# Scatters in pairs and singly between the splits' operations, a reordered filling stage, and one ACT write for both choices' rows

## The reference

```
x = layernorm(x + attn(x))       # 16 heads of 8, q/k/v through V (8x8), softmax over 512 keys, back through U and Wo
x = layernorm(x + ffn(x))        # gate: softmax over 8 experts, top 2, renormalised
                                 # expert: relu(x @ w1.T + b1) @ w2.T + b2, hidden size 512
```

## Time and profile before

| | |
|---|---|
| median of 3 runs | 1258.94 us (1251.39 to 1264.15) |
| the profiled execution: time | 1257.38 us |
| its span, first to last instruction | 1255.6 us |
| mean granted clock of PE | 0.939 |
| busy: PE, DVE, ACT, POOL | 86%, 78%, 72%, 47% of the span |
| first exponential scores (L553) / last | 76.3 / 904.6 us |
| L799 DVE row maxima | 512 of 1220 ns |
| L685 ACT exponentials | 512 of 1023 ns |

### The profile page before, as it was taken

The page is one execution under the profiler, slowest core; times in us unless marked ns, Lnnn a source line. Parts: engine busy times, 40 slices in busy tenths (PEclk is TensorE's granted clock), DMA queues, the critical chain, the costliest instruction groups (busy, mean ns, idle before and its releaser), DMA issues. The chain is left out here.

```text
span 1255.6 us, 24757 instructions
## 1 busy us (share of the span) xinstructions
PE 1082.8 (86%) x7711; PEld 520.5 (41%) x7711; DVE 975.3 (78%) x2117; ACT 904.2 (72%) x1177; POOL 586.5 (47%) x823
## 2 busy tenths in 40 slices
PE   3578998989889898898988999888728999999977
PEld 2222222222222222222222222222218999999952
DVE  4578888989778797887988879797146888888845
ACT  1157877778677786867878678687618999999927
POOL 1314316255271642626336263323254777777745
PEclk9989999999899998989999899899758999999989
DMA  3733133141331413223142231400012222222246
GB/s 80 235 94 90 49 101 89 54 132 42 95 92 51 126 37 106 73 67 102 43 127 69 71 97 36 122 15 19 14 51 63 69 68 69 69 69 71 66 159 257
DMA packets 105461, 104.88 MB, mean 84 GB/s; under 512 B 21608, under 2 KB 82834, under 8 KB 105376
## 3 DMA queue, kind: packets, MB, share of 16 engines
q1 hardware_dynamic: 94912, 81.88, 22.5%
q0 software_dynamic: 8448, 16.93, 4.2%
q10 hardware_dynamic: 2016, 4.98, 1.1%
HBM read 56.06 MB, written 47.39 MB: 82 GB/s over the span
## 5 line engine op out<-in xcount | busy, mean ns | idle before, releaser
L799 DVE TENSOR_REDUCE row_max<-score_ps 128x2 f32<-128x1024 f32 x512 | 618.0, 1220 | 138.9 <-PE score_ps L571 91.3
L685 ACT ACTIVATE probs<-score_ps 128x1024 f32<-128x1024 f32 x512 | 521.6, 1023 | 157.4 <-PE score_ps L553 132.6
L534 PE MATMUL av_ps<-probs,v_one 128*9 128x512 f32 x2048 | 285.2, 630 | 7.9 <-ACT probs L685 6.5
L571 PE MATMUL score_ps<-k_stack,q_stack 48*128 48x512 bf16 x1024 | 207.5, 402 | 75.2 <-ACT probs L685 57.5
L553 PE MATMUL score_ps<-q_stack,k_stack 51*128 51x512 bf16 x1024 | 205.7, 399 | 22.0 <-DVE row_max L799 15.1
L371 POOL TENSOR_TENSOR max_parts<-neg_max,zeros 32x128 bf16<-32x128 f32 x32 | 14.2, 445 | 386.9 <-ACT neg_max L623 386.9
L1096 ACT ACTIVATE w_cur<-experts 128x1156 f32 x136 | 158.5, 1167 | 37.5 <-PEq L413 17.2
L553 PEld LDWEIGHTS score_ps<-q_stack,k_stack 51*128 51x128 bf16 x1024 | 49.2, 93 | 320.4 <-issue 154.2
L1192 POOL DMA_INDIRECT y_d<-y_out,place x136 | 136.8, 1006 | 44.7 <-issue 44.7
L846 POOL DMA_INDIRECT routed_d<-rows,slot_i x128 | 125.4, 980 | 67.2 <-issue 36.9
L1053 PE MATMUL up_ps<-xt_sb,w_cur 128*128 128x128 f32 x1088 | 146.2, 278 | 0.0
(11 more groups left out here) (187 smaller groups left out, 1153.3 us busy)
## 6 DMA issues: line engine op xcount, KB each, us to landing
k_stack<-k_stack_d SPq DMA_DIRECT2D x128, 96.0 KB, 2.4
q_stack<-q_stack_d SPq DMA_DIRECT2D x128, 96.0 KB, 2.5
x_rows_sb<-routed_d SPq DMA_DIRECT2D x136, 65.0 KB
q_stack_d<-q_parts SPq DMA_DIRECT2D x32, 192.0 KB
k_stack_d<-k_parts SPq DMA_DIRECT2D x30, 192.0 KB
x_in<-L_attn_x SPq DMA_DIRECT2D x16, 256.0 KB, 3.1
q_stack_d<-q_parts SPq DMA_DIRECT2D x32, 128.0 KB
x_res<-L_attn_x SPq DMA_DIRECT2D x16, 256.0 KB, 3.1
```

What stands on the lines that cost most here:

```text
L534: last = nc.tensor.matmul(av_ps[32 * g:32 * g + V_COLS, :], v_one[n.parity][:, kb, HG * hg + g, :], probs[:, (2 * j + g // 2) % P_RING, g ...
L571: last = nc.tensor.matmul(max_bank(b, s)[:, a, :], q_stack[n.parity][at, c, g * P:(g + 1) * P], k_stack[n.parity][at, c, :], start=True, s ...
L685: nc.scalar.activation(probs[:, s % P_RING, :, :], exp_bank(b, s)[:, :, :], ACT.Exp).then_inc(S["exp_done"], 1)
L799: nc.vector.tensor_reduce(row_max[:, m // (STEPS // 2), :, m % (STEPS // 2)], max_bank(b, s)[:, :, :], AX.X, ALU.max).then_inc(S["red_done ...
```

## The change

1. **Scatters.** On POOL scatters 0 and 1 now stand ahead of `split_max(b, 1)`, 2 and 3 right behind it, 4 between the second and third operation of q's split, 5 behind that split, 6 between the second and third operation of k's split and 7 behind it. None is left beside `split_max(n1, 0)`. The last batches, which have no q and k to split, have them in one piece.
2. **SP.** `max_rows(n1, 0)` is issued ahead of the wait for the stored parts and of `stacks(n2, 0)` and `(n2, 1)`.
3. **Filling stage.** The experts stand at steps 24 to 31, one in each step. The two banks have their own counts, so that PE can fill one while ACT copies the other. On POOL `split_max(0, 0)` comes between the splits of q and k of batch 1, and on SP its `max_rows` between their stores.
4. **ACT.** L617 writes both choices at once (input 128x128, output 128x256), in steps 18 to 21. The copy L671 and its semaphore are gone.

```diff
...

-EXPERT_AT = [STEPS - 2 * (E - e) for e in range(E)]
-SCALE_AT = 16
+EXPERT_AT = [STEPS - E + e for e in range(E)]
+SCALE_AT = 17
 LEAST = -3.0e38
...
          "xt_sb q_sb k_sb ynt_sb y_ready exp_done "
-         "x1t_done x1t_sb logits_done logits_sb second_sb top_step rank_done slot_step place_out copied "
+         "x1t_done x1t_sb logits_done logits_sb second_sb top_step rank_done slot_step place_out "
          "red_done negmax_sb yn_inv yn_sb v_sb res_ready stats_ready mv_ready x1_ready "
...

-def split(engine, queue, full, parts, rest_t, zeros, part_ready, value, last_sem):
+def split(engine, queue, full, parts, rest_t, zeros, part_ready, value, last_sem, between=None):

...
     engine.tensor_tensor(rest_t, full, parts[:, 0, :], ALU.subtract).then_inc(part_ready, 1)
+    if between:
+        between()
     queue.wait_ge(part_ready, value(2))
...

-def split_q(engine, queue, n):
+def split_q(engine, queue, n, between=None):
     queue.wait_ge(S["q_sb"], n.count(1, 1))
...
     wait(queue, S["split_done"], n.count(2, 0))
-    split(engine, queue, q_f[:, :], q_parts, rest[:, :], zeros[:, :], S["qpart_ready"], lambda k: n.count(3, k), S["split_done"])
-
-def split_k(engine, queue, n):
+    split(engine, queue, q_f[:, :], q_parts, rest[:, :], zeros[:, :], S["qpart_ready"], lambda k: n.count(3, k), S["split_done"], between)
+
+def split_k(engine, queue, n, between=None):
     queue.wait_ge(S["k_sb"], n.count(1, 1))
     queue.wait_ge(S["split_done"], n.count(2, 1))
-    split(engine, queue, k_f[:, :], k_parts, rest[:, :], zeros[:, :], S["kpart_ready"], lambda k: n.count(3, k), S["split_done"])
+    split(engine, queue, k_f[:, :], k_parts, rest[:, :], zeros[:, :], S["kpart_ready"], lambda k: n.count(3, k), S["split_done"], between)

...
                     pe.wait_ge(experts_loaded, 32)
+                wait(pe, experts_copied, 2 * e - 1)
+                for h in range(HB):
+                    last = nc.tensor.transpose(score_ps[2][:, 0, h * P:(h + 1) * P], w1_n[:, e * HB + h, :], ident[:, :])
+                last.then_inc(experts_ps, 1)
                 wait(pe, experts_copied, 2 * e)
                 for h in range(HB):
-                    nc.tensor.transpose(score_ps[2][:, 0, h * P:(h + 1) * P], w1_n[:, e * HB + h, :], ident[:, :])
                     last = nc.tensor.transpose(score_ps[2][:, 1, h * P:(h + 1) * P], w2_n[:, e, h * P:(h + 1) * P], ident[:, :])
...
                     wait(act, scattered[n.parity], n.count_parity(8 * 16, 0))
-                nc.scalar.activation(rows[n.parity][:, 0, t, 0:D], res[:, t, :], ACT.Identity, bias=shift[:, t:t + 1],
+                nc.scalar.activation(rows[n.parity][:, :, t, 0:D], res[:, t, :].unsqueeze(1).to_broadcast([P, 2, D]), ACT.Identity, bias=shift[:, t:t + 1],
                                      scale=rstd[:, t:t + 1]).then_inc(S["x1_ready"], 1)
...
             def copy_expert(e):
-                act.wait_ge(experts_ps, e + 1)
+                act.wait_ge(experts_ps, 2 * e + 1)
                 nc.scalar.activation(experts[:, e, W1], score_ps[2][:, 0, :], ACT.Copy).then_inc(experts_copied, 1)
+                act.wait_ge(experts_ps, 2 * e + 2)
                 nc.scalar.activation(experts[:, e, W2], score_ps[2][:, 1, :], ACT.Copy).then_inc(experts_copied, 1)
...
                     neg(n1, 0)
-                if s == 25 and prev:
-                    act.wait_ge(S["x1_ready"], p1.count(QT, QT))
-                    nc.scalar.activation(rows[p1.parity][:, 1, :, 0:D], rows[p1.parity][:, 0, :, 0:D], ACT.Copy).then_inc(S["copied"], 1)
                 if s == 28 and prev:
...
                                         ALU.add).then_inc(S["xbo_ready"], 1)
-            if cur:
-                split_max(b, 1)
             if prev2:
...
                 pool.wait_ge(S["slot_step"], p2.count(SLOT_STEPS, SLOT_STEPS))
-                pool.wait_ge(S["copied"], p2.count(1, 1))
+                pool.wait_ge(S["x1_ready"], p2.count(QT, QT))
                 scatter(p2, 0, 2)
+            if cur:
+                split_max(b, 1)
+            if prev2 and cur:
+                scatter(p2, 2, 4)
             if prev:
...
                 nc.gpsimd.tensor_tensor(shift[:, :], minus_mean[:, :], rstd[:, :], ALU.mult).then_inc(S["shift_ready"], 1)
+            spread = prev2 and cur and proj
+            if prev2 and cur and not proj:
+                scatter(p2, 4, 8)
             if proj and not is_first(b):
-                split_q(nc.gpsimd, pool, n2)
-                split_k(nc.gpsimd, pool, n2)
-            if prev2:
-                scatter(p2, 2, 6)
-            if nxt:
+                split_q(nc.gpsimd, pool, n2, (lambda: scatter(p2, 4, 5)) if spread else None)
+                if not cur:
+                    split_max(n1, 0)
+                if spread:
+                    scatter(p2, 5, 6)
+                split_k(nc.gpsimd, pool, n2, (lambda: scatter(p2, 6, 7)) if spread else None)
+                if spread:
+                    scatter(p2, 7, 8)
+            if cur and nxt:
                 split_max(n1, 0)
-            if prev2:
-                scatter(p2, 6, 8)
+            if prev2 and not cur:
+                scatter(p2, 2, 8)

...
                 store_parts(sp, q_stack_d[n2.parity], q_parts, Q_PLACES)
+            if nxt and not cur:
+                max_rows(n1, 0)
             if proj and not is_first(b):
...
                 store_parts(sp, k_stack_d[n2.parity], k_parts, K_PLACES)
+            if cur and nxt:
+                max_rows(n1, 0)
             if proj:
...
                 stacks(n2, 1)
-            if nxt:
-                max_rows(n1, 0)
             if proj:```

The order of instructions shows three of the places. The first is POOL's queue in the body of b = 3, from the first operation of q's split. `routed_d<-rows,slot_i` is a scatter. Before:

```order
L371 TENSOR_TENSOR q_parts<-q_f,zeros 128x512
L373 TENSOR_TENSOR rest<-q_f,q_parts 128x512
L375 TENSOR_TENSOR q_parts<-rest,zeros 128x512
L377 TENSOR_TENSOR q_parts<-rest,q_parts 128x512
L371 TENSOR_TENSOR k_parts<-k_f,zeros 128x512
L373 TENSOR_TENSOR rest<-k_f,k_parts 128x512
L375 TENSOR_TENSOR k_parts<-rest,zeros 128x512
L377 TENSOR_TENSOR k_parts<-rest,k_parts 128x512
L846 DMA routed_d<-rows,slot_i 66688x130 x4
L371 TENSOR_TENSOR max_parts<-neg_max,zeros 32x128
```

## The result

The changed kernel takes 1182.45 us (median of 4 runs, 1181.73 to 1185.48) against 1261.18 us (1251.39 to 1264.15) for the kernel before: a ratio of 0.939, with a 95% interval of 0.934 to 0.945. Lines of the code are numbered a little higher now: the negation is L628, the scaling L622, the scores L555, the maxima L573, DVE's row maximum L802, ACT's exponential L688.

A forecast was written before the change was run, and what follows sets the result against it. It took the attention stage to be bound by PE held where scatters meet k's stores, with a slow clock behind. -53 + 6 - 4 - 6 = -57 from 1257.38 gave 1200 us, range 1186 to 1250.

The forecast's parts named there:

- The holds: PE held about 2 us near step 25 in 12 bodies, by scatters beside k's stores; ending them: -53 us.
- B: Rival: the hold shrinks with the scatters in it, half of holds and slow stretches staying; 1226 us, chance 0.15.
- C: Rival: any scatter beside the stores is enough, or something unchanged holds PE; 1248 us, chance 0.14.
- the first scores: Filling stage: the first scores would come at about 70.2 us in place of 76.26.
- the negation: Filling stage: the negation behind the third expert would come at about 63 us in place of 68.85.
- A period of 48.5 us: Attention stage: each of 13 periods between negations at step 26 falls to 48.5 us; -53 us in all.
- Late max rows, +6: Step 0: max rows, behind a later k's store, come 0.5 us late in each of 12 batches; +6 us.
- The copy, 0.3 us in each batch: ACT: dropping L671 ahead of step 26's exponential saves 0.3 us in each of 14 batches; -4 us.
- Filling stage, -6: Before the first batch: experts at later steps bring the first scores earlier; -6 us, bounds -3 and -9.
- A: The forecast itself: one scatter beside the stores does not hold PE; 1187 to 1214 us, chance 0.52.
- D: Rival: two scatters beside q's stores hold PE, twice in each of 12 bodies; 1301 us, chance 0.07.
- E: Rival: max rows come late, PE waits 1.66 us at every step 0, with slow clock; 1232 us, chance 0.09.

The follow-up runs named there:

- e7: Changed kernel with scatters 4 to 7 together behind k's split, beside k's stores, in 12 bodies; 1239.72 us, ratio 0.981 to the kernel before.
- e5: Kernel before with the new order of scatters and SP's new order, old copy and filling stage; 1197.51 us, ratio 0.949.
- e1: Kernel before with the new order of scatters alone; 1274.60 us, ratio 1.013.
- e3: Kernel before with the reordered filling stage alone; 1249.32 us, ratio 0.993.
- e4: Kernel before with SP's new order alone; 1254.98 us, ratio 0.996.
- e2: Kernel before with ACT's one write of both choices alone, the copy gone; 1252.16 us, ratio 0.995.
- e15: Changed kernel with the old filling stage; 1193.52 us, ratio 0.948 to the kernel before.
- e6: Changed kernel with scatters 6 and 7 together behind k's split; 1183.04 us, ratio 0.937 to the kernel before.
- e11: Changed kernel with scatters 4 to 7 together behind the split of the next batch's maxima; 1213.56 us, ratio 0.962 to the kernel before.
- e8: Changed kernel with scatters 4 to 7 together behind q's split, ahead of k's split; 1198.31 us, ratio 0.950 to the kernel before.
- e12: Kernel of e7 with SP's stores of k's parts issued after the max rows; 1187.54 us, ratio 0.945 to the kernel before.
- e9: Changed kernel with four more direct DMAs to a scratch area behind scatter 7 in 12 bodies; 1190.95 us, ratio 0.945 to the kernel before.
- e13: Changed kernel with scatters 4 and 5 behind k's split, 6 and 7 behind the next maxima's split; 1192.96 us, ratio 0.948 to the kernel before.

## Why the prediction was right or wrong

**Right: what was lost before, and that the change ends it.** The holds were the cost, and they needed scatters and a burst of SP together. e7 puts them back by the place of four scatters alone, and 57 of the 79 us are lost again. The changed kernel has no remote wait at all, which excludes B and C. The wide reading of the Trainium skill's rule ("SBUF — State Buffer", who interferes with whom) that a DMA never contends with a compute engine falls too: with the same DMAs and the same bytes, PE's semaphores come 2 us late or not, by where four scatters stand. That page speaks of SBUF ports, and no run shows that ports are what delays PE. What I had not foreseen is that three scatters together are as free as one.

**Right: the first scores** (69.92 against 70.2 forecast) and the negation (62.59 against 63).

**The step that failed: the sum, -57 against -75.3 in the spans.** The mechanism was right and the terms were too small. Two of them make most of it: +6 us for late max rows, where PE lost nothing to them, and the last batch, which was left out without a reason and gave 5.3 us. By its terms:

- *A period of 48.5 us, from 50.91 less PE's idle 2.4.* With the copy still there e5 has 48.28: a hold in a body without slow clock takes up to 2.6 us with it, a little more than the wait of PE that the profile shows. 13 x 0.22 = 2.9 us too little. The period that I had started from also held the meeting of DVE and POOL at 272.03 shown above, which I had not seen.
- *Late max rows, +6.* Measured: none. The rows were there when I had said (the issue ended at 257.81, 23.8 us after the layer norm's first operation at 234.05, and 1.34 for the landing makes 25.1; forecast 25.0). But the scores came 25.3 after it, not 24.6. A balance of two times within 1 us of each other should have been given as zero with a bound, not as a term.
- *The copy, 0.3 us in each batch.* The trace has 0.42 (48.28 in e5, 47.86 in the changed kernel): 1.5 us more. That is also more than ACT's work became less, 0.64 - 4 x 0.11 = 0.20. What counted was the copy's place, right ahead of an exponential that PE waits for; the dearer scaling stands where there is slack.
- *Filling stage, -6.* By step 10 of the first batch it was -8.3 (83.90 against 92.18). The 2.3 us are a slow clock, from 75 to 82 us, behind PE's wait of 3.56 us in the earlier trace rows. I had read that price of a pause for the holds and forgotten it here.
- *The last batch* was not in the sum. From its negation to the last scores it took 57.2 us before and 51.9 now. In the one before the granted clock is at the lower level from 894.2 to 904.4. To its last exponential it takes 57.4 to 57.6 us in before, e1, e3 and e4, which have the copy, and 52.3 to 53.0 in e2, e7, e15 and the changed kernel without it, but 54.5 in e5 with it, and 54.4 in e6 and 56.2 in e11 without it. So it is not the copy alone. What decides it stays open.

2.9 + 6 + 1.5 + 2.3 + 5.3 = 18.0 of the 18.3 us.

The range failed with the sum. The low end of 1186 us was called the lower bounds of A, but the bounds that the terms had been given add up to -62 + 0 - 6 - 9 = -77, or 1180 us. The late rows, the copy and the filling stage came out at or near their own lower bounds (0, -5.5 and -8.3), the periods, with the copy still in them, at -56 (13 x 48.28 against 683.6), between -53 and -62. The measured 1182 lies above that 1180, though the last batch is in none of the terms.

**The rivals.** D, a hold at q's stores, is real in kind: four scatters do it (e8). But the two that the change puts there do not, and the price there is about 1 us a body, where the clock did not fall, and not 4.4. E, late max rows, is real too, and far larger than I had it, if SP's order is not changed with the scatters (e1: 59 us). I had priced SP's new order as a nicety worth 1.66 us. It is what turned a loss of 1.3% into a gain of 5.1%. This did not move the forecast, which had both orders in it, but it was luck that they were changed together: I had costed the scatters' delay of k's stores only with the new order, and never asked what the old one would have made of it.

## What to carry to other kernels

Where a profile shows several engines waiting for PE by "remote" at one moment, look at what the DMA queues do there, and try to move the indirect DMAs apart: here three in a row were free and four cost 4.8 us a time. When work is inserted ahead of a transfer, follow the transfer's queue down to the last thing that waits behind it; a queue's order that did not matter can become the bound. And price a wait of PE with the slow clock behind it: holds of some 2.4 us were worth 2.6 us at most with no slow clock behind them, and 3.6 to 6.2 with it.

## What the runs showed of the hardware

- Four indirect DMAs of 128 rows of 520 bytes, issued every 1.26 us while SP's queue moves data, delay what PE should have finished: DVE's waits for it were 2.4 us each on average in e7, 1.2 in e8 and 0.7 to 1.2 in e11. In e7 the scores and the maxima, which should be done at 255.32 and 255.54, were released to ACT and DVE together at 257.6. Two or three do not, nor do two and two, four direct ones of the same shape do not, and four with SP's bursts behind them do not (e12's traced run). What in the chip does it, and whether PE's array or only its signals stand still, the profile does not show.
- POOL issues a direct DMA of this shape in 0.56 us (2.22 for 4, e9), an indirect one in 0.96, with 0.30 ahead of the next (e7).
- PE's granted clock fell to the lower level behind PE's pauses of 2.48 us, 2.59 (e7) and 6.11 (e1), not behind one of 2.38 at 267.20 in the kernel before, nor behind the one of 1.16 us in e8. So a pause went ahead of each of these falls, but its length alone did not decide in these rows.
- DVE's TENSOR_TENSOR on 128x32 took 1.19 us in place of 0.19 beside POOL's on 128x512: in 12 batches of e13 (1.19 to 1.20), and in three of the kernel before (1.16 to 1.19).
